# A two-layer attention and feed-forward kernel: scores between gate and up products, attention four query tiles later, values projected in step 15

## The chip, the cores and the metric

The kernel runs on one core of one Trainium2 chip. The metric is the device time of one execution in microseconds (us), median of the runs. TensorE (PE) multiplies matrices out of SBUF into the eight PSUM banks; VectorE (DVE), ScalarE (ACT) and GpSimd (POOL) work on the results; SyncE (SP) issues the DMAs. Each engine executes its own instructions in the order in which they are written, and waits on semaphores where it needs another engine's result.

## The reference

```python
x = L0_attn_x                                     # 4 batches x 512 tokens x 512, f16
xn = _layernorm(x)
s = _L0_attn_ref(xn, Wq, Wk, Wv, Wo)              # 32 query heads, 8 key/value heads of 16, softmax(q k^T / 4) v, then Wo
g = _silu(_L0_ffn_ref(xn, SU_ug, SU_dp, Wscale_ug, Wscale_dp, W_up, W_gate, W_down))
x = x + s * g
...
# _L0_ffn_ref
x = fwht(x * SU_ug) / SCALE
x_up = x @ W_up.T * (Wscale_ug[:INTER] * SCALE)       # INTER = 2048
x_gate = x @ W_gate.T * (Wscale_ug[INTER:] * SCALE)
x = jax.nn.silu(x_gate) * x_up
x = fwht(x * SU_dp) / SCALE
x = x @ W_down.T * (Wscale_dp * SCALE)
```

A second layer follows (a gated linear recurrence and a feed-forward with signs of weights, each again multiplied and added to x). The change touches only layer 0.

## The kernel before

The Walsh-Hadamard transforms are moved onto the weights. Layer 0 is one loop over steps `t` (`TEND` of them), written out once for every engine; `BSTEPS` is 64, so `b, m = t // 64, t % 64` are the batch and the step in it.

**Attention.** A unit `u` is one key/value head of one batch (32 units), with its four query heads. A tile is one unit and 128 query rows: four matmuls (`scores`, one for each query head, 32 rows of contraction, 512 columns) fill the four banks `SC_`; DVE takes the four row maxima (`row_max`, `top_n`), ACT the four exponentials (`exps`, `probs`), SP turns the tile by a DMA transpose (`turn_probs`), and `weigh` multiplies two turned tiles with the values (16 short matmuls). There are 128 tiles, numbered 0 to 127. `scores` of a tile waits until all four exponentials of the tile before have been read out of the banks. After a unit, DVE turns the result (`to_tokens`), divides (`divide`, partly POOL) and, once for two units, turns it back (`to_features`). Before the change tile k stands in step 2k, `weigh` in steps with t % 4 == 0.

**Preparation.** In steps 0 to 31 PE transforms the gate and up weights (`transform_ug`, two f32 products into one of the two banks `GB`), ACT makes the high half (`high_half`), DVE the low half (`low_half`), which frees the bank; POOL does the first level of the butterfly (`chunk_pairs`), four steps to a chunk. The normalised inputs of batches 1 to 3 are turned through one bank `MISC` (`turn_x`, `evict_x`) in the ten steps of `TURN_STEP` from 9 on and in two before. The down weights are taken through butterflies on POOL (`dn_pair`, steps 16 to 61) and through `transform_dn` on PE (the steps `DN_AT`, 49 to 68).

**Gate and up products.** In steps m = 32 to 63 of a batch, `ffn` computes one product per step, eight matmuls of 512 columns into one of the two `GB` banks: even steps gate, odd steps up. ACT takes the tanh of the gate (`tanh_gate`), DVE multiplies (`gate_mul`, which frees the gate's bank, then `up_mul`, which frees the up bank and writes `row32`), ACT copies the high half of `row32` (`high_rows`), POOL writes the low half (`low_rows`), and only then may the next `up_mul` overwrite `row32`. `tanh_gate` waits for the `up_mul` before it, since both use `tg`. `ahead` says how many matmuls of a step's product stand before the scores.

**Down products.** In steps m = 0 to 31 of the next batch (for the last one, t = 256 to 287, with no attention before the change) six matmuls per step; `scale_down`, `tanh_down`, `second_gate`, `project_o` (steps `OUT_STEP`), `gated`, `residual` finish a block of 128 tokens. `project_q`, `project_k` and `project_v` for what comes next use the bank `MISC` too.

**Tail.** At t = 256 SP issues the loads of layer 1 (`tail_constants`: the first batch `nx`, the weights `wst`, eleven constants). At m = 3 of that stretch DVE executes `next_stats`, `weight_max(0)`, `next_scale`, `weight_max(1)` and `weight_maxima` in one piece, each waiting for its load. From m = 11 on SP loads raw weights into `probs`, `probsT` and `rows` (`load_raw`, the first waits for the last `weigh`), ACT writes their signs (`raw_sign`, eight of them), PE turns and projects (`turn_next`, `project_next`), and layer 1 begins when all engines have ended layer 0.

Of the kernel before, what the change touches and what calls it, by code (L numbers as in the profile page):

```python
# [34 lines left out]
TOKEN_STEP, DIVIDE_STEP, TURN_BACK = 4, 6, 2  # L35
GATE_AHEAD, DOWN_AHEAD = (4, 3), (1, 0)
LATE_EVICT = 70
# [3 lines left out]
OUT_STEP = (17, 19, 28, 35)  # L41
OUT_LAST = (17, 21, 28, 35)
NEXT_STEP, EVICT_STEP = 19, 20
XRES_STEP = (17, 19, 24, 25)
Q_STEP, V_STEP, K_STEP = 5, 43, 49
# [112 lines left out]
def layer0(nc, d, x1_dram, W):  # L158

    ctx = ExitStack()  # L160
    with ctx:  # L161
# [113 lines left out]
        def _(sp):  # L275
# [83 lines left out]
            for t in range(TEND):  # L359
                b, m = t // BSTEPS - 1, t % BSTEPS  # L360
                if t % 2 == 0 and 0 <= t // 2 - 1 < NU * TT:
                    turn_probs(t // 2 - 1)
# [11 lines left out]
                if t % STEPS == 6 and t // STEPS + 2 < NU:  # L374
                    load_k(t // STEPS + 2)
                if t % STEPS == 2 and 1 < t // STEPS + 1 < NU:
                    load_q(t // STEPS + 1)
# [15 lines left out]
        def _(pool):  # L393
# [81 lines left out]
            for t in range(TEND):  # L475
# [36 lines left out]
        def _(v):  # L512
# [277 lines left out]
            for t in range(TEND):  # L790
# [27 lines left out]
                if b < B and m > FFN_STEP and m % 2:  # L818
                    gate_mul(b, (m - FFN_STEP) // 2)
                if t % 2 and 0 <= (t - 3 - FFN_STEP) // 2 < LOW_FIRST:  # L820
                    low_rows((t - 3 - FFN_STEP) // 2)
                if t % STEPS == TOKEN_STEP and 0 <= t // STEPS - 1 < NU:
                    to_tokens(t // STEPS - 1)
                if t % STEPS == DIVIDE_STEP and 0 <= t // STEPS - 1 < NU:
                    divide(t // STEPS - 1)
                if t % STEPS == TURN_BACK and 0 <= t // STEPS - 2 < NU and t // STEPS % 2:
                    to_features(t // STEPS - 2)
# [22 lines left out]
        def _(a):  # L850
# [137 lines left out]
            for t in range(TEND):  # L988
# [1633 lines left out]
```

## Time and profile before

| | |
|---|---|
| median of 3 runs | 1391.0 us (1390.41 to 1392.87) |
| profiled execution, its time / its span | 1391.33 us / 1389.4 us |
| busy share over the span | PE 91%, DVE 76%, ACT 56%, POOL 38% |
| granted TensorE clock over the span, of full speed | 0.982 |
| first scores / start of step 32 / start of step 256 / start of layer 1, in the trace | 25.07 / 158.60 / 694.55 / 759.86 us |

Times in the trace count from the span's start. A row of the timeline gives start, length, engine, line, operation, what is written and read, and a count where equal neighbours are merged; in square brackets stands how long the engine was idle before it and whose result ended that. A row of the windows gives, for a stretch, its length and each engine's busy time with the number of its instructions, then the granted TensorE clock, the busy share of the DMA engines and GB/s. A busy PE is an average over stages in which different things end the waits.

### The profile page before, as it was taken

To read this page: it belongs to the slowest core of one execution; us is meant where nothing else is said; L and a number is where in the kernel's file an instruction comes from. 1 tells how busy PE (TensorE), PEld (TensorE's weight loads), DVE (VectorE), ACT (ScalarE), POOL (GpSimd) and SP (SyncE) were. 2 spreads that over 40 slices of the span, in tenths; PEclk is the share of its full clock that TensorE was granted. 3 is DMA by queue.
4 is the path that set the end of the run, shared out by engine and by line. 5 is a ranking of instruction groups with operands and counts; after the bars stand their busy time and mean duration, and the time that the engine had idled before them with its cause. 6 is when DMAs were issued, how large, how long until landed. Compare 5 with 4: busy or idle time off the path is not lost. (4 is left out here: it accounts for less than half of the span.)

```text
span 1389.4 us, 23478 instructions
## 1 busy us (share of the span) xinstructions
PE 1263.2 (91%) x8738; PEld 637.2 (46%) x8738; DVE 1055.3 (76%) x1823; ACT 783.0 (56%) x1308; POOL 524.6 (38%) x434
## 2 busy tenths in 40 slices
PE   4667788888998999998898999999999999999998
PEld 2222233333333333333343555855477555855475
DVE  7765886778887888778863976968956976968946
ACT  5665666666776677667726752355433652355431
POOL 3369865211220132013201663328431573328431
PEclk9898999999999999999999999999999999999999
DMA  6864563577777876877675024001131024001121
GB/s 233 204 143 96 96 107 73 96 145 152 121 117 144 164 122 113 149 160 115 119 260 212 1 59 92 17 31 37 44 72 39 8 59 92 17 31 37 43 43 46
DMA packets 346561, 135.59 MB, mean 98 GB/s; under 512 B 312176, under 2 KB 333392, under 8 KB 343888
## 3 DMA queue, kind: packets, MB, share of 16 engines
q1 hardware_dynamic: 334032, 132.52, 44.1%
q10 hardware_dynamic: 12416, 1.57, 1.0%
q8 instruction: 70, 1.15, 0.4%
q14 instruction: 43, 0.35, 0.1%
HBM read 44.87 MB, written 17.87 MB: 45 GB/s over the span
## 5 line engine op out<-in xcount | busy, mean ns | idle before, releaser
L1157 PE MATMUL bank<-rows,both 128*128 128x512 f16 x1024 | 245.9, 383 | 28.6 <-DVE tg L644 19.8
L638 DVE TENSOR_REDUCE top_n<-vpair 128x1 f32<-128x512 f32 x256 | 164.8, 686 | 102.0 <-PE bank L1126 101.8
L940 ACT ACTIVATE probs<-vpair,top_n 128x512 f16<-128x512 f32 x256 | 164.4, 687 | 109.1 <-DVE top_n L638 109.0
L1171 PE MATMUL bank<-dn,h 128*128 128x512 f16 x768 | 179.8, 383 | 4.3 <-DVE fd L711 2.5
L1157 PEld LDWEIGHTS bank<-rows,both 128*128 128x128 f16 x1024 | 91.3, 98 | 164.8 <-DVE tg L644 43.4
L638 DVE TENSOR_REDUCE top_n<-bank 128x1 f32<-128x512 f32 x256 | 163.7, 682 | 0.0
L940 ACT ACTIVATE probs<-bank,top_n 128x512 f16<-128x512 f32 x256 | 162.9, 690 | 0.0
L454 POOL TENSOR_TENSOR h<-th,h 128x512 f16<-128x512 f32 x61 | 70.5, 1155 | 192.5 <-ACT h L909 192.5
L2239 PE MATMUL bank<-rows,both 128*128 128x512 f16 x512 | 118.5, 382 | 0.0
L1171 PEld LDWEIGHTS bank<-dn,h 128*128 128x128 f16 x768 | 71.5, 99 | 98.3 <-issue 15.9
L2255 PE MATMUL bank<-both,hid 128*128 128x512 f16 x512 | 111.2, 379 | 0.0
L2223 PE MATMUL bank<-rows,both 128*128 128x512 f16 (+1 forms) x456 | 104.0, 379 | 0.9 <-PEq L161 0.9
L2255 PEld LDWEIGHTS bank<-both,hid 128*128 128x128 f16 x512 | 50.0, 98 | 60.5
L467 POOL TENSOR_TENSOR otok<-oblk,rl 128x256 f16<-128x256 f32 x25 | 15.5, 619 | 155.3 <-DVE rl L684 155.3
L2239 PEld LDWEIGHTS bank<-rows,both 128*128 128x128 f16 x512 | 48.4, 100 | 55.5 <-issue 1.1
L909 ACT ACTIVATE h<-th 128x512 f16<-128x512 f32 x64 | 40.3, 629 | 51.5 <-DVE th L657 51.5
L2223 PEld LDWEIGHTS bank<-rows,both 128*128 128x128 f16 (+1 forms) x456 | 43.7, 98 | 55.5 <-issue 4.4
L1614 POOL TENSOR_TENSOR big<-big,both 128x384 f32<-128x384 f32 x32 | 32.0, 1026 | 94.4 <-DMA big<-t_scratch 70.7
L1126 PE MATMUL vpair<-qk 32*128 32x512 f16 x256 | 51.2, 396 | 13.1 <-ACT probs L940 12.9
L1568 POOL TENSOR_TENSOR hid<-sil 128x512 f32<-128x512 f32 x24 | 33.1, 1379 | 62.5 <-DVE sil L1688 62.5
L657 DVE SCALAR_TENSOR_TENSOR th<-bank,hsc,tg 128x512 f32<-128x512 f32 x64 | 48.0, 750 | 9.8 <-DMA x_scratch<-th 6.8
L1628 POOL TENSOR_TENSOR os_<-os_,both 128x6 f32<-128x6 f32 x16 | 23.3, 1458 | 80.6 <-DVE os_ L1986 80.6
(358 smaller groups left out, 2559.3 us busy)
## 6 DMA issues: line engine op xcount, KB each, us to landing
h<-in_ug SPq DMA_DIRECT2D x8, 1024.0 KB, 6.3
lt_scratch<-big SPq DMA_DIRECT2D x16, 384.0 KB, 2.7
dn<-in_down SPq DMA_DIRECT2D x2, 2048.0 KB, 11.0
x_scratch<-th SPq DMA_DIRECT2D x16, 256.0 KB, 2.7
res<-x_scratch SPq DMA_DIRECT2D x16, 256.0 KB, 4.3
out_x<-res SPq DMA_DIRECT2D x16, 256.0 KB, 2.0
both<-in_w SPq DMA_DIRECT2D x2, 1548.0 KB, 11.8
t_scratch<-tok SPq DMA_DIRECT2D x16, 192.0 KB, 2.1
```

The costliest lines, as they stand in the source:

```text
L454: pool.tensor_tensor(h16(ft, 1), row32, h16(ft, 0), ALU.subtract).then_inc(S["row_lo"], 1)
L638: v.tensor_reduce(top_n[:, i:i + 1], SC_[n % G][:, :], AX.X, ALU.max, negate=True).then_inc(S["max_done"], 1)
L657: v.scalar_tensor_tensor(row32, GB[n % 2][:, :], hsc[:, ft:ft + 1], tg[:, :], ALU.mult, ALU.mult).then_inc(S["gb_took"], 1)
L909: a.activation(h16(ft, 0), row32, ACT.Copy).then_inc(S["row_hi"], 1)
L940: a.activation(probs[:, k % TAKEN, j * T:(j + 1) * T], SC_[j][:, :], ACT.Exp, bias=top_n[:, i:i + 1]).then_inc(S["p_ready"], 1)
L1126: pe.matmul(SC_[j][:, :], qs[32 * j:32 * j + 32, u % SLOTS, qt * P:(qt + 1) * P], ks[32 * j:32 * j + 32, u % SLOTS, :], start=True, stop=T ...
L1157: mm = pe.matmul(GB[n % 2][:, :], w[:, kt, col:col + P], xnb(b, kt), start=r == 0, stop=r == 2 * KT - 1)
L1171: mm = pe.matmul(bk, h16(ft, r // 2)[:, rows], dn16(ft, r % 2), start=j == 0 and r == 0, stop=j == FT - 1 and r == 2)
L1568: pool.tensor_tensor(sqf[m % 2], sil[:, ORDER[m], :], sil[:, ORDER[m], :], ALU.mult).then_inc(S["sq_r"], 1)
L2223: mm = pe.matmul(bk, lhs(i, kt), rhs(j, kt), start=n == 0, stop=n == 3 * KT - 1)
L2239: mm = pe.matmul(fbank[ht % 2][:, :], up[:, kt, ht * P:(ht + 1) * P], x_half(i, kt), start=kt == 0 and i == 0, stop=kt == KT - 1 and i == 1)
L2255: mm = pe.matmul(fbank[tt % 2][:, :], hid[:, i, ht, tt * P:(tt + 1) * P], down[:, ht, :], start=ht == 0 and i == 0, stop=ht == HT - 1 and ...
```

## The change

Attention moves by `ATT = 8` steps (four tiles) and by one step in parity: tile k now stands in step 2k + 9, an odd one, between the gate product of the even step and the up product of the odd one. `weigh` stands in steps with t % 4 == 1, there with one up matmul ahead of the scores. The first eight steps hold no attention, and tiles 124 to 127 fall in steps 257 to 263, into the down products of the last batch. In the preparation `transform_ug` goes behind the scores on PE, and `high_half` behind the exponentials and `evict_x` on ACT. `gate_mul` moves between the first and the second row maximum, `up_mul` behind the fourth; `high_rows` goes between the first and the second exponential. `project_v` goes from step 43 to 15, `project_k` from 49 to 57, the output projections from 17 and 19 (17 and 21 for the last batch) to 20 and 22; `evict_q`, `evict_v`, `evict_k` always one step later than their product. No operation is added or dropped.

```diff
+ATT = 8
-TOKEN_STEP, DIVIDE_STEP, TURN_BACK = 4, 6, 2
-GATE_AHEAD, DOWN_AHEAD = (4, 3), (1, 0)
-LATE_EVICT = 70
+TOKEN_STEP, DIVIDE_STEP, TURN_BACK = 6, 0, 2
-OUT_STEP = (17, 19, 28, 35)
-OUT_LAST = (17, 21, 28, 35)
+OUT_STEP = (20, 22, 28, 35)
+OUT_LAST = (20, 22, 28, 35)
-Q_STEP, V_STEP, K_STEP = 5, 43, 49
+Q_STEP, V_STEP, K_STEP = 5, 15, 57
...
@@ SP
-                if t % 2 == 0 and 0 <= t // 2 - 1 < NU * TT:
-                    turn_probs(t // 2 - 1)
+                ta = t - ATT
+                if ta % 2 == 0 and 0 <= ta // 2 - 1 < NU * TT:
+                    turn_probs(ta // 2 - 1)
...
@@ DVE
-                if t > FFN_STEP + 1 and (t - 2) // BSTEPS < B and (t - 2) % BSTEPS >= FFN_STEP and t % 2 == 0:
-                    up_mul((t - 2) // BSTEPS, ((t - 2) % BSTEPS - FFN_STEP) // 2)
-                if t < NU * STEPS and t % 2 == 0:
-                    for j in range(G):
-                        row_max(2 * t + j)
+                ta = t - ATT
+                paired = ta % 2 and 0 <= ta // 2 < NU * TT
+                if paired:
+                    row_max(G * (ta // 2))
+                if b < B and m > FFN_STEP and m % 2:
+                    gate_mul(b, (m - FFN_STEP) // 2)
+                if paired:
+                    for j in range(1, G):
+                        row_max(G * (ta // 2) + j)
+                if t % 2 and 0 <= (t - 3 - FFN_STEP) // 2 < LOW_FIRST:
+                    low_rows((t - 3 - FFN_STEP) // 2)
+                if b < B and m > FFN_STEP and m % 2:
+                    up_mul(b, (m - FFN_STEP) // 2)
...
@@ ACT
                 if b < B and m > FFN_STEP and m % 2:
                     tanh_gate(b, (m - FFN_STEP) // 2)
+                if paired:
+                    exps(G * (ta // 2))
+                if 0 <= fb < B and fm > FFN_STEP and t % 2:
+                    high_rows(fb, (fm - FFN_STEP) // 2)
+                if paired:
+                    for j in range(1, G):
+                        exps(G * (ta // 2) + j)
+                if t in TURN_STEP:
+                    evict_x(KT + TURN_STEP.index(t))
                 if 0 <= t - PREP - 2 < NCH * KT:
                     high_half(t - PREP - 2)
-                if t < NU * STEPS:
-                    exps(2 * t)
-                    exps(2 * t + 1)
-                if t in TURN_STEP:
-                    evict_x(KT + TURN_STEP.index(t))
...
@@ PE
+                ta = t - ATT
+                ahead = 1 if ta % 4 == 1 else 0
                 if t in TURN_STEP:
                     turn_x(KT + TURN_STEP.index(t))
+                ffn(t, 0, ahead)
+                if ta % 2 and 0 <= ta // 2 < NU * TT:
+                    scores(ta // 2)
+                if ta % 4 == 1 and 0 <= ta // 4 - 2 < 2 * NU:
+                    weigh(ta // 4 - 2)
                 if 0 <= t - PREP - 2 < NCH * KT:
                     transform_ug(t - PREP - 2)
-                ahead = 0
-                if t % 2 == 0:
-                    ahead = (DOWN_AHEAD if m < FFN_STEP else GATE_AHEAD)[t // 2 % 2]
-                ffn(t, 0, ahead)
-                if t < NU * STEPS and t % 2 == 0:
-                    scores(t // 2)
-                if t % 4 == 0 and 0 <= t // 4 - 2 < 2 * NU:
-                    weigh(t // 4 - 2)
                 ffn(t, ahead, 2 * KT)
```

On DVE, in the gate and up stretch of the last batch before the change (L638 is `row_max`, L644 `gate_mul`, L657 `up_mul`, L676 `to_tokens`, L684 the reciprocal of `divide`):

```order
L638 TENSOR_REDUCE top_n<-vpair 128x1 x2
L638 TENSOR_REDUCE top_n<-bank 128x1 x2
L676 STREAM_TRANSPOSE oblk<-bank 128x512
L644 SCALAR_TENSOR_TENSOR tg<-tg,bank 128x512
L657 SCALAR_TENSOR_TENSOR th<-bank,hsc,tg 128x512
L638 TENSOR_REDUCE top_n<-vpair 128x1 x2
L638 TENSOR_REDUCE top_n<-bank 128x1 x2
L684 RECIPROCAL rl<-oblk 128x16
L644 SCALAR_TENSOR_TENSOR tg<-tg,bank 128x512
L657 SCALAR_TENSOR_TENSOR th<-bank,hsc,tg 128x512
```

The same place of the changed kernel:

```order
L638 TENSOR_REDUCE top_n<-vpair 128x1
L644 SCALAR_TENSOR_TENSOR tg<-tg,bank 128x512
L638 TENSOR_REDUCE top_n<-vpair 128x1
L638 TENSOR_REDUCE top_n<-bank 128x1 x2
L657 SCALAR_TENSOR_TENSOR th<-bank,hsc,tg 128x512
L676 STREAM_TRANSPOSE oblk<-bank 128x512
L638 TENSOR_REDUCE top_n<-vpair 128x1
L644 SCALAR_TENSOR_TENSOR tg<-tg,bank 128x512
L638 TENSOR_REDUCE top_n<-vpair 128x1
L638 TENSOR_REDUCE top_n<-bank 128x1 x2
L657 SCALAR_TENSOR_TENSOR th<-bank,hsc,tg 128x512
L684 RECIPROCAL rl<-oblk 128x16
```

`gate_mul` no longer stands behind the four maxima and the unit's own operations, but behind the first maximum; the unit's operations stand behind `up_mul`.

On DVE around step 259 (m = 3 of the last stretch), before the change, from the last `up_mul` on (L766 to L734 are `next_stats` to `weight_maxima`, L711 is `scale_down`):

```order
L657 SCALAR_TENSOR_TENSOR th<-bank,hsc,tg 128x512
L766 BN_STATS both<-rows 128x6 x4
L769 BN_AGGR both<-both 128x2 x4
L771 TENSOR_SCALAR both<-both 128x4
L727 TENSOR_REDUCE both<-both 128x1
L776 TENSOR_SCALAR rows<-rows,both 128x512 x4
L727 TENSOR_REDUCE both<-both 128x1
L733 TENSOR_TENSOR both<-both 128x1
L734 TENSOR_REDUCE both<-both 128x1
L676 STREAM_TRANSPOSE oblk<-bank 128x512
L684 RECIPROCAL rl<-oblk 128x16
```

The same place of the changed kernel, from tile 125 on:

```order
L638 TENSOR_REDUCE top_n<-vpair 128x1 x2
L638 TENSOR_REDUCE top_n<-bank 128x1 x2
L766 BN_STATS both<-rows 128x6 x4
L769 BN_AGGR both<-both 128x2 x4
L771 TENSOR_SCALAR both<-both 128x4
L727 TENSOR_REDUCE both<-both 128x1
L776 TENSOR_SCALAR rows<-rows,both 128x512 x4
L727 TENSOR_REDUCE both<-both 128x1
L733 TENSOR_TENSOR both<-both 128x1
L734 TENSOR_REDUCE both<-both 128x1
L638 TENSOR_REDUCE top_n<-vpair 128x1 x2
L638 TENSOR_REDUCE top_n<-bank 128x1 x2
```

The row maxima of tiles 126 and 127, which stood ahead of this piece, now stand behind it.

On PE in steps 10 and 11 of the preparation before the change, from the turn of step 10 on (L1046 is `turn_x`, L1067 and L1068 `transform_ug`, L1126 the scores, L1057 a sum of maxima):

```order
L1046 MATMUL bank<-ident,both 128x128 x4
L1067 MATMUL bank<-h,had 128x512
L1068 MATMUL bank<-h,nhad 128x512
L1126 MATMUL vpair<-qk 128x512 x2
L1126 MATMUL bank<-qk 128x512 x2
L1046 MATMUL bank<-ident,both 128x128 x4
L1067 MATMUL bank<-h,had 128x512
L1068 MATMUL bank<-h,nhad 128x512
```

The same steps of the changed kernel (its lines of PE are eight higher):

```order
L1054 MATMUL bank<-ident,both 128x128 x4
L1075 MATMUL bank<-h,had 128x512
L1076 MATMUL bank<-h,nhad 128x512
L1054 MATMUL bank<-ident,both 128x128 x4
L1134 MATMUL vpair<-qk 128x512 x2
L1134 MATMUL bank<-qk 128x512 x2
L1075 MATMUL bank<-h,had 128x512
L1076 MATMUL bank<-h,nhad 128x512
```

The scores stand in step 11 and ahead of its transform.

## Rows read from the trace of the kernel before

**Rows 1.** Windows: preparation, gate/up and down stretches, the tail.

```profile
25.07:57.66 32.59, 22.52 (x66) 8.46 (x66) 25.24 (x42) 25.39 (x41) 12.15 (x6) 0.90 0.72 234
57.66:158.60 100.94, 69.19 (x295) 25.19 (x296) 66.81 (x116) 60.26 (x104) 74.81 (x57) 0.87 0.61 124
158.60:256.22 97.62, 84.94 (x498) 33.45 (x497) 76.67 (x121) 66.58 (x111) 60.20 (x50) 0.98 0.49 88
325.88:406.57 80.69, 72.99 (x478) 29.18 (x478) 67.85 (x109) 59.94 (x100) 21.93 (x21) 1.00 0.71 125
406.57:470.67 64.10, 58.77 (x407) 23.96 (x408) 49.81 (x84) 43.09 (x70) 6.06 (x8) 1.00 0.81 149
615.15:694.55 79.40, 70.20 (x454) 27.22 (x453) 67.66 (x110) 58.71 (x97) 21.34 (x20) 1.00 0.73 125
694.55:719.24 24.69, 22.20 (x129) 9.87 (x129) 14.49 (x23) 0.65 (x2) 2.71 (x5) 1.00 0.89 303
719.24:759.86 40.62, 35.08 (x168) 15.25 (x168) 21.14 (x34) 26.87 (x21) 5.75 (x6) 0.92 0.53 200
```

**Rows 2.** Who waited for whom, up to 800 us: in total, times, longest.

```profile
ACT probs L940 <- DVE top_n L638: 109.0, 112, 4.7
DVE top_n L638 <- PE bank L1126: 101.8, 106, 3.5
```

**Rows 3.** Timeline of the preparation, about 73 us and 149 us.

```profile
73.41 0.69 ACT L890 ACTIVATE both<-bank,suc 128x512 f16<-128x512 f32 x1 [3.09 <-PE bank L1068]
75.80 0.38 PE L1057 MATMUL bank<-amax,allone 128*128 128x1 f32 x2 [2.42 <-ACT rows L872]
...
149.16 1.13 PE L1067 MATMUL bank<-h,had 128*128 128x512 f32 x2 [1.36 <-DVE both L627]
150.13 1.02 PE L1068 MATMUL bank<-h,nhad 128*128 128x512 f32 x2
```

**Rows 4.** Timeline of one tile's interval in the second gate/up stretch.

```profile
358.33 0.39 PE L1126 MATMUL vpair<-qk 32*128 32x512 f16 x2
358.75 1.29 DVE L638 TENSOR_REDUCE top_n<-vpair 128x1 f32<-128x512 f32 x2 [0.66 <-PE bank L1126]
359.21 2.76 PE L1157 MATMUL bank<-rows,both 128*128 128x512 f16 x12
359.48 1.28 ACT L940 ACTIVATE probs<-vpair,top_n 128x512 f16<-128x512 f32 x2 [0.72 <-DVE top_n L638]
360.66 0.68 ACT L952 ACTIVATE tg<-bank,usc 128x512 f32<-128x512 f32 x1
361.78 0.65 DVE L644 SCALAR_TENSOR_TENSOR tg<-tg,bank 128x512 f32<-128x512 f32 x1
362.47 0.75 DVE L657 SCALAR_TENSOR_TENSOR th<-bank,hsc,tg 128x512 f32<-128x512 f32 x1
362.49 0.82 PE L1157 MATMUL bank<-rows,both 128*128 128x512 f16 x3 [0.52 <-DVE tg L644]
363.24 0.39 PE L1126 MATMUL vpair<-qk 32*128 32x512 f16 x2
363.25 0.63 ACT L909 ACTIVATE h<-th 128x512 f16<-128x512 f32 x1 [0.27 <-DVE th L657]
363.96 1.16 POOL L454 TENSOR_TENSOR h<-th,h 128x512 f16<-128x512 f32 x1 [3.98 <-ACT h L909]
```

**Rows 5.** Timeline of the tail: load of nx, block's end, raw loads, last sign.

```profile
697.40 0.53 SPq L327 DMA_DIRECT2D rows<-x_scratch  x1
710.11 0.45 SPq L345 DMA_DIRECT2D probs<-in_upw  x1
717.07 0.71 DVE L676 STREAM_TRANSPOSE oblk<-bank 128x512 f32<-128x512 f32 x1
719.24 0.61 PE L1171 MATMUL bank<-dn,h 128*128 128x512 f16 x1 [2.49 <-DVE fd L711]
755.25 1.91 ACT L971 ACTIVATE both<-probsT 128x2048 f16<-128x2048 f32 x1 [0.40 <-DMA probsT<-in_downw]
```

More of the change, by code:

```diff
@@ L373, in _ @@
                     load_chunk((t - PREP - 2) // 4 + 2)
[L374 to L377, printed above, removed]
+                if ta % STEPS == 6 and 1 < ta // STEPS + 2 < NU:
+                    load_k(ta // STEPS + 2)
+                if ta % STEPS == 2 and 1 < ta // STEPS + 1 < NU:
+                    load_q(ta // STEPS + 1)
                 if b >= 0 and m in XRES_STEP:
@@ L503, in _ @@
                 fb, fm = (t - 2) // BSTEPS, (t - 2) % BSTEPS
-                if fb < B and fm >= FFN_STEP and t % 2 == 0 and (fb or (fm - FFN_STEP) // 2 >= LOW_FIRST):
+                if fb < B and fm >= FFN_STEP and t % 2 and (fb or (fm - FFN_STEP) // 2 >= LOW_FIRST):
                     low_rows(fb, (fm - FFN_STEP) // 2)
-                if t % STEPS == DIVIDE_STEP and t // STEPS - 1 in POOL_UNITS:
-                    divide(t // STEPS - 1)
+                if (t - ATT) % STEPS == DIVIDE_STEP and (t - ATT) // STEPS - 2 in POOL_UNITS:
+                    divide((t - ATT) // STEPS - 2)
                 if b and m - 2 in out_step(b):
@@ L817, in _ @@
                     bound_scales()
[L818 to L827, printed above, removed]
+                if ta % STEPS == TOKEN_STEP and 0 <= ta // STEPS - 1 < NU:
+                    to_tokens(ta // STEPS - 1)
+                if ta % STEPS == DIVIDE_STEP and 0 <= ta // STEPS - 2 < NU:
+                    divide(ta // STEPS - 2)
+                if ta % STEPS == TURN_BACK and 0 <= ta // STEPS - 2 < NU and ta // STEPS % 2:
+                    to_features(ta // STEPS - 2)
                 if b == B and m == 3:
@@ L993, in _ @@
                     normalise(3)
-                if t > FFN_STEP + 1 and (t - 2) // BSTEPS < B and (t - 2) % BSTEPS >= FFN_STEP and t % 2 == 0:
-                    high_rows((t - 2) // BSTEPS, ((t - 2) % BSTEPS - FFN_STEP) // 2)
+                ta = t - ATT
+                paired = ta % 2 and 0 <= ta // 2 < NU * TT
+                fb, fm = (t - 2) // BSTEPS, (t - 2) % BSTEPS
                 if b < B and m > FFN_STEP and m % 2:
                     tanh_gate(b, (m - FFN_STEP) // 2)
+                if paired:
[7 more added lines that the diff above has]
+                    evict_x(KT + TURN_STEP.index(t))
                 if 0 <= t - PREP - 2 < NCH * KT:
                     high_half(t - PREP - 2)
-                if t < NU * STEPS:
-                    exps(2 * t)
-                    exps(2 * t + 1)
-                if t in TURN_STEP:
-                    evict_x(KT + TURN_STEP.index(t))
                 for ft in range(FT):
@@ L1007, in _ @@
                         magnitudes(ft)
+                if t % 16 == Q_STEP + 1 and t // 16 + 1 < NU // 2:
+                    evict_q(t // 16 + 1)
+                if m == V_STEP + 1 and b + 1 < B:
+                    evict_v(b + 1)
+                if m == K_STEP + 1 and b + 1 < B:
+                    evict_k(b + 1)
                 if t in DN_AT:
                     high_down(DN_AT.index(t))
-                late = 1 if t < LATE_EVICT else 2
-                if t % 16 == Q_STEP + late and t // 16 + 1 < NU // 2:
-                    evict_q(t // 16 + 1)
-                if m == V_STEP + late and b + 1 < B:
-                    evict_v(b + 1)
-                if m == K_STEP + late and b + 1 < B:
-                    evict_k(b + 1)
                 if b and m - 1 in DOWN_END:
```

1 line of the change is left out of this document (added).

## The prediction

> **What bounds the kernel now.** I read the windows by stretch first. Layer 1 (from 759.86 us on) is not touched and starts when layer 0 ends, so only the stretches of [rows 1] count. The reader should see three kinds. In the two stretches of the preparation PE is busy 69% of the time at a granted clock of 0.87 to 0.90 (between its two levels, 1.2 and 2.4 GHz), DVE and ACT 60 to 78%: nobody is full, the steps hang on a ring of waits. In the gate and up stretches PE is busy 88 to 90% and DVE 84%; in a down stretch PE 92%. In the tail PE is full until 716.75 us, waits 2.49 us, and then is busy 86% at clock 0.92. The list of waits, second, says what the ring is: ACT waits 109.0 us for row maxima and DVE 101.8 us for scores [rows 2]: one tile of attention in flight at a time.
>
> The ring of one tile, third, from the timeline [rows 4]. S is the start of a tile's scores. The first row maximum starts at S + 0.42 (358.75), the others 0.60 apart (the second pair starts 1.21 after the first), the first exponential 0.73 after the first maximum, the others 0.60 apart and 0.68 long. Without anything between, the last exponential ends at 0.42 + 0.73 + 3 x 0.60 + 0.68 = S + 3.63, and the next scores can start at S + 3.68. In the row they start at S + 4.91, and not for the exponentials: DVE had four maxima, a unit's operation (0.62 to the next start) and then `gate_mul` (361.78), and PE sat 0.52 us until it freed the gate's bank, then did three matmuls. So before the change a gate/up interval is 0.42 + 4 x 0.60 + unit's operation + 0.65 + 0.05 + three or four matmuls (0.213 apart: 12 take 2.76) with 0.1 behind them: 4.5 to 5.1. The mean is 4.81: the last batch's stretch of 16 tiles is 79.40 [rows 1], 4.96 each, of which I put 2.4 us in all to its start and its one projection.
>
> **Step 1: steps 0 to 7, no attention.** Before, 32.59 us [rows 1]. Left are the transforms: 0.97 + 0.9 = 1.9 us on PE at full clock [rows 3], `high_half` 0.69, `low_half` 0.75, two banks. In the first four steps DVE has the statistics and the first `chunk_max` of about 2.3 each and ACT four normalisations (some 3): I work out 11.4 us; in the next four a chain of 1.9 + 0.69 + 0.75 for two steps and a `chunk_max`, 9.2. Sum 20.6, so **-12**. Bounds: 16 us if only PE's transforms count, 28 if only the exponentials and maxima of four tiles (4.8 us less of waiting) go.
>
> **Step 2: steps 8 to 31.** Before 100.94 us [rows 1], twelve double steps of 8.41. What held them is seen in [rows 3]: ACT idle 3.09 us until PE's transform, then `high_half`, two exponentials, `evict_x`, and PE idle 2.42 us until that `evict_x`: PE and ACT take turns, since ACT has `high_half` ahead of exponentials and `evict_x`. Afterwards scores go ahead of the transform and `evict_x` ahead of `high_half`, so PE transforms while DVE and ACT work on the tile. A double step without turns then takes: first maximum to last exponential 3.20, `high_half` twice 0.69 + 0.60, `low_half` 0.75 (DVE has it ahead of the next maxima), hand-overs 0.15: 5.4; I take 6.0. With turns it is ACT's work: four exponentials 3.1, two `evict_x` 1.2, two `high_half` 1.3, 2.7 magnitudes 1.7: 7.3, I take 7.6. Five double steps with turns, seven without, and 1.0 for each of six chunks (`chunk_max` stands between maxima and `low_half`): 38 + 42 + 6 = 86. So **-15**. Bounds: POOL is busy 74.81 us in this stretch and can't be passed, -26; no gain, 0; a loss is a rival below.
>
> **Step 3: gate and up stretches.** The new ring. DVE has `gate_mul` after the first maximum: 0.60 more, so the exponentials end at S + 4.23 and the scores could follow at S + 4.28; `high_rows` fits in the pause this leaves on ACT. PE: after the scores 0.88 (with `weigh`) or 0.33, then 16 matmuls: 4.2 or 3.8, hidden. The gate was full before the scores, so its tanh (0.68) is done in time. But `up_mul` waits for POOL: first exponential S + 1.14, `high_rows` at 1.74 for 0.63, POOL at 2.45 for 1.16, `up_mul` at 3.65 for 0.75: its bank is free at S + 4.45. Where one up matmul stands ahead of the next scores (every second tile) these start at 4.45 + 0.31 = S + 4.76. A unit's transpose (0.62 in a pause of 0.4) adds 0.24 in three of eight tiles. Mean: (4.28 + 4.76) / 2 + 0.09 = 4.61. Sixteen tiles: 73.8. Three projections, now in steps with `weigh` where PE is full (0.88 + 3.4 + 0.85 + hand-over = 5.3 for 4.28), 1.0 each; output projection 0.4; first double step 1.0. Batches 1 and 2: 78.2 against 80.69, **-2.5** each. Last batch, one projection: 76.2 against 79.40, **-3.2**. Batch 0, 97.62 [rows 1]: the first half gains about 3; in the second `transform_dn` in both steps of a pair makes a ring through `low_rows`, `up_mul`, two `low_down`s of 7.6 us, and `project_k` now stands among them: +2. **-1**. Moving `project_v` out saves nothing more: PE was waiting there for `gate_mul`. Bounds for the mean interval: 4.37 (PE alone with `weigh` half the time) to 4.81, or -15 to +13 us over 64 tiles.
>
> **Step 4: down stretches.** 64.10 us for 16 tiles of 3.68 and projections [rows 1]. The ring is unchanged. `project_v` comes in at m = 15, +0.6; the output projections at 20 and 22 with `project_q` at 21 wait one for the other through `MISC` (`gated` stands behind the maxima of step 21), about 3.6 lost, as much as before. **+0.5** each, three of them: +1.5.
>
> **Step 5: the tail.** T0 is the start of step 256: before, 694.55, and layer 1 starts at T0 + 65.3. Now SP issues the load of `nx` behind the turn of tile 123, 2.85 us after its exponentials as before, at S + 7.1 (S: tile 123, T0 = S + 2.0). DVE's piece of step 259 ended 19.67 us after that issue (697.40 to 717.07 [rows 5]), which nobody but PE's 2.49 us felt. Now the maxima of tile 126 stand behind it: S + 26.8. Scores of tile 127 at S + 26.8 + 3.2 = S + 30. PE could be there at S + 15.2 (three tiles of 3.68, twelve matmuls and `weigh`) and is in order: all down products wait behind, **14.8 us of stall**. Then 54 matmuls and two `weigh`, 13.4, and 1.6 at the lower clock: step 272 at T0 + 43.0, before T0 + 24.7 [rows 1]: +18.3. After that PE had 40.62 us for what, by busy time and clock (35.08 x 0.92), is 32.3 of work; it waited for DVE and ACT, which are now ahead. I take 34.3, 6.3 given back: **+12**. Bounds: +9 (all given back) to +26 (below). The 1.6 is half of the 3.2 us of clock lost in the last window (0.08 x 40), where PE was idle for long twice.
>
> By the Trainium skill, TensorE: Matmul & The Clock Gate (section HAM oscillation — how this bites in real kernels), idle gaps of PE bring the clock down, which speaks against this change; the last window's 0.92 agrees. The page's 426.7 ns against 215.7 ns for 512 columns (section Wait — 56ns, not 53.3ns?) would make it an estimated 2.5 us if the twelve matmuls behind the stall ran slow, and the sum 0.9 higher.
>
> **Sum.** -12 - 15 - 1 - 2.5 - 2.5 - 3.2 + 1.5 + 12 = -22.7. From the profiled execution's own 1391.33 us (span 1389.4 and 1.9 around it; 0.3 above the median): 1368.6, say **1369**.
>
> **Rivals.** *The signs become the end of layer 0.* `load_raw` waits for the last `weigh`, now at S + 43.5. Before, the last sign ended 47.05 us after the first raw load (710.11 to 757.16 [rows 5]) and layer 1 started 2.7 later. Kept whole, that is T0 + 91: +26 for +12, **1383**. Against it: then the first sign had waited for other work, not for its load. *The product ring gains nothing:* `up_mul` through POOL also holds back the tiles without an up matmul ahead, mean 4.81: 64 x 0.20 = +13, **1382**. *Everything fits better:* the interval is PE's 4.37: -15, **1354**. *It doesn't do what it says:* the stretches keep their lengths and tail and start cancel, **1391**. *Slower: the preparation goes serial.* With scores ahead of the transform, at the lower clock: scores to last exponential 3.8, `evict_x` 0.6, turn 0.4, a transform at 1.2 GHz (not quite twice the 1.9) 3.3, `high_half` 0.7, `low_half` 0.75, 9.6 in all per double step, for 7.2, +29: **1398**. It decides against the change above 7.2 + 22.7 / 12 = 9.1 us, more than today's 8.41. For it: clock 0.87 there, and every bank is single. Against: only turns force this order.
>
> **Numbers.** Forecast 0.50 (its own range 1360 to 1378), signs 0.14, product ring 0.10, better 0.09, no change 0.05, serial preparation 0.12. A measurement tells from no change what is above 0.2%, 2.8 us. Faster 0.83, same 0.05, slower 0.12. The range reaches from the better case to beyond the signs: 1354 to 1388.
>
> **What would show it.** First scores about 48 us; step 32 about 131 instead of 158.6; gate/up stretches of 76 to 78; intervals that alternate 4.3 and 4.8; POOL's wait for `high_rows` smaller, `up_mul` waiting for POOL; PE idle about 15 us once in the last 70 us of layer 0, ended by an exponential; lower clock behind it. Wrong it would be made above all by a double step in the preparation far from 7.2, or a tail that keeps all of its 18.

## The result, and the profile after

The changed kernel takes **1399.8 us** (median of 4 runs, 1399.38 to 1404.37), the kernel before 1390.7 beside it. The ratio is 1.0068, 95% interval 1.0046 to 1.0091: slower by 0.7%, where 1369 was predicted. The profiled execution of after took 1404.37 us (span 1402.6), 13.0 more than the one of before and 4.6 above its own median; between the medians lie 9.1.

I cut both traces at the scores of the same steps (of before, tile 16 in step 32, and so on; of after, tile 12 in step 33). The windows of after, with the columns of [rows 1]: preparation, gate and up of batch 0, gate and up of batch 1, down stretch behind it, gate and up of the last batch, and the tail in two parts, up to the scores of tile 127 and to layer 1.

```profile
49.08:135.58 86.50, 62.33 (x281) 25.03 (x280) 65.33 (x112) 61.90 (x107) 72.74 (x54) 0.94 0.52 115
135.58:241.70 106.12, 88.43 (x484) 34.59 (x484) 77.74 (x123) 67.21 (x109) 63.05 (x53) 0.92 0.47 84
315.12:403.01 87.89, 74.90 (x464) 29.91 (x464) 66.19 (x107) 61.13 (x99) 20.29 (x19) 0.94 0.62 114
403.01:469.69 66.68, 59.66 (x423) 24.84 (x425) 50.20 (x86) 43.76 (x72) 7.68 (x9) 1.00 0.79 143
622.75:702.15 79.40, 71.23 (x456) 28.73 (x456) 66.02 (x107) 60.27 (x97) 20.30 (x19) 0.98 0.69 126
702.15:726.02 23.87, 10.15 (x79) 4.15 (x80) 20.61 (x33) 7.89 (x13) 3.32 (x6) 0.85 0.93 278
726.02:772.91 46.89, 46.35 (x258) 20.82 (x258) 26.35 (x44) 29.38 (x25) 5.76 (x5) 0.97 0.69 236
```

The account in us, after less before: start of the first gate and up stretch 135.58 - 158.60 = **-23.0**; gate and up of batch 0 106.12 - 97.62 = **+8.5**, of batch 1 87.89 - 80.69 = **+7.2**, of batch 2 **+6.6**, of batch 3 79.40 against 79.40; the three down stretches +3.8, +2.6, +2.0; from the scores of tile 124 to layer 1 70.76, where before step 256 to layer 1 took 65.31: **+5.4**. Sum +13.1. The preparation gained what was forecast, and everything behind it but the last batch's gate and up stretch lost it again. The +8.5 of batch 0 is partly this one execution: in four other runs that keep its code there (third, sixth, seventh and eighth below) the stretch takes 101.4 to 105.0 us for 106.12. The clock points the same way: 0.94 in batch 1's gate and up stretch, 1.00 before [rows 1].

The list of waits up to 800 us, total, times, longest:

```profile
ACT probs L944 <- DVE top_n L638: 140.9, 131, 13.6
DVE top_n L638 <- PE bank L1134: 70.4, 74, 5.3
ACT kst L920 <- DMA qk<-qst: 19.7, 3, 7.2
```

DVE waits less for scores than in [rows 2], ACT more for maxima. The third row is short and the telling one: three waits of up to 7.2 us, one in each of batches 0 to 2, of `evict_k` for a load of queries. Before, the same three waits came to 3.6 us in all.

Undisturbed tiles run as predicted. Three starts of scores on PE in the second gate and up stretch, `gate_mul` (L644) and `up_mul` (L657, released by POOL's `low_rows`, L454) on DVE between them:

```profile
338.59 0.39 PE L1134 MATMUL vpair<-qk 32*128 32x512 f16 x2
339.62 0.68 DVE L644 SCALAR_TENSOR_TENSOR tg<-tg,bank 128x512 f32<-128x512 f32 x1
342.32 0.75 DVE L657 SCALAR_TENSOR_TENSOR th<-bank,hsc,tg 128x512 f32<-128x512 f32 x1 [0.23 <-POOL h L454]
342.87 0.39 PE L1134 MATMUL vpair<-qk 32*128 32x512 f16 x2
346.59 0.75 DVE L657 SCALAR_TENSOR_TENSOR th<-bank,hsc,tg 128x512 f32<-128x512 f32 x1 [0.22 <-POOL h L454]
347.40 0.39 PE L1165 MATMUL bank<-rows,both 128*128 128x512 f16 x1 [0.58 <-DVE th L657]
347.72 0.39 PE L1134 MATMUL vpair<-qk 32*128 32x512 f16 x2
```

4.28 us from scores to scores, then 4.85 where an up matmul stands ahead of them and waits for `up_mul`, as in the working (4.28 and 4.76). The largest losses lie in single intervals. The first kind, from the scores of tile 57 (m = 59 of batch 1) to those of tile 58, in the timeline of all engines:

```profile
381.59 0.39 PE L1134 MATMUL vpair<-qk 32*128 32x512 f16 x2
382.01 0.69 DVE L638 TENSOR_REDUCE top_n<-vpair 128x1 f32<-128x512 f32 x1 [1.03 <-PE bank L1134]
384.20 2.44 SPq L320 DMA_DIRECT2D qk<-qst  x4
387.96 0.60 ACT L920 ACTIVATE kst<-bank 128x512 f16<-128x512 f32 x1 [7.23 <-DMA qk<-qst]
388.45 0.68 ACT L956 ACTIVATE tg<-bank,usc 128x512 f32<-128x512 f32 x1
389.02 0.69 ACT L944 ACTIVATE probs<-vpair,top_n 128x512 f16<-128x512 f32 x1
389.91 4.02 PE L1165 MATMUL bank<-rows,both 128*128 128x512 f16 x9 [6.09 <-DVE tg L644]
393.86 0.61 PE L1134 MATMUL vpair<-qk 32*128 32x512 f16 x2
```

`evict_k` stands in step m = 58 on ACT and overwrites keys that the loads of heads read; it waits for the last unit's queries, which SP issues in that same step (L320). The tanh of step 59 and the exponentials of tile 57 stand behind it on ACT; DVE waits for the tanh, PE 6.09 us for DVE. Then nine matmuls take 4.02 us, 0.45 each, where twelve undisturbed ones take 2.76, 0.23 each [rows 4]: the clock has fallen (0.75 granted over this interval). The interval is 12.27 us; without the wait it is 4.86 (second experiment). By the Trainium skill, TensorE: Matmul & The Clock Gate (section HAM oscillation — how this bites in real kernels), a PE idle gap is paid a second time through the clock; the trace agrees with these two numbers.

Before the change the eviction was no further from that load in steps: the same step in batch 0, one step behind it in batches 1 and 2. But the four exponentials of tile 57 stood between the two on ACT, and its wait was 1.16 us. In the timeline of before:

```profile
374.29 2.79 SPq L321 DMA_DIRECT2D qk<-qst  x4
375.99 1.27 ACT L940 ACTIVATE probs<-bank,top_n 128x512 f16<-128x512 f32 x2
378.41 0.60 ACT L916 ACTIVATE kst<-bank 128x512 f16<-128x512 f32 x1 [1.16 <-DMA qk<-qst]
```

Now the load is issued behind the turn of tile 56, at 384.20, and ACT has nothing in between: it stands idle from 380.73 on. So by these rows the move laid the wait open by what it took from between the load and the eviction on ACT, not by bringing them into one step.

The second kind, at the first double step of batch 1's gate and up products (timeline):

```profile
318.73 0.58 SPq L388 DMA_DIRECT2D x_scratch<-th  x1
321.52 0.75 DVE L657 SCALAR_TENSOR_TENSOR th<-bank,hsc,tg 128x512 f32<-128x512 f32 x1 [2.90 <-DMA x_scratch<-th]
322.33 3.14 PE L1165 MATMUL bank<-rows,both 128*128 128x512 f16 x8 [2.43 <-DVE th L657]
322.36 0.69 ACT L956 ACTIVATE tg<-bank,usc 128x512 f32<-128x512 f32 x1 [2.51 <-DVE th L657]
```

`up_mul` shares its buffer with the rows of block 2 that are being stored, and now stands in step 33 instead of 34; it waits 2.90 us for the store, and tanh and PE wait for it. With the transposes and the output projection behind it the interval is 9.15 us. This wait is not new. The kernel before has it in the same three stretches, 6.8 us in all for 9.1 here; its row at the start of batch 1's products:

```profile
332.76 0.75 DVE L657 SCALAR_TENSOR_TENSOR th<-bank,hsc,tg 128x512 f32<-128x512 f32 x1 [2.52 <-DMA x_scratch<-th]
```

There the first three intervals of the stretch take 18.0 us, in the changed kernel 18.6.

The tail: load of `nx`, DVE's piece, the maxima of tile 126 behind it, the scores of tile 127, `weight_low`, a tanh of the down products (L964), the first sign.

```profile
703.91 1.12 SPq L326 DMA_DIRECT2D rows<-x_scratch  x1
710.31 2.47 DVE L766 BATCH_NORM_STATS2 both<-rows 128x6 f32<-128x512 f32 x4 [1.14 <-DMA rows<-x_scratch]
722.77 1.28 DVE L638 TENSOR_REDUCE top_n<-vpair 128x1 f32<-128x512 f32 x2
726.02 0.60 PE L1134 MATMUL vpair<-qk 32*128 32x512 f16 x2 [12.65 <-ACT probs L944]
736.50 7.06 DVE L751 SCALAR_TENSOR_TENSOR both<-both 128x1548 f16<-128x1548 f32 x4 [0.94 <-ACT both L969]
747.26 0.63 ACT L964 ACTIVATE th<-fd 128x512 f32<-128x512 f32 x1 [6.27 <-DVE fd L711]
747.80 1.89 ACT L975 ACTIVATE both<-probs 128x2048 f16<-128x2048 f32 x1
```

The stall of tile 127 is there, 12.65 us for the 14.8 predicted; the granted clock over its window is 0.85. What it costs is another question (below).

### The profile page after: what moved, and what is told of

It is laid out like the page before. It is cut to its first block and busy times, and to the rows that moved or that the text cites. A ratio compares the mean times of both kernels' runs of the same rounds, so it can differ in the third digit from the quotient of the medians.

```text
span 1402.6 us, 23475 instructions
## 1 busy us (share of the span) xinstructions
PE 1261.8 (90%) x8738; PEld 642.9 (46%) x8738; DVE 1049.7 (75%) x1823; ACT 787.3 (56%) x1306; POOL 525.1 (37%) x434
## 5 line engine op out<-in xcount | busy, mean ns | idle before, releaser
L1165 PE MATMUL bank<-rows,both 128*128 128x512 f16 x1024 | 252.3, 393 | 40.6 <-DVE th L657 24.6
L944 ACT ACTIVATE probs<-vpair,top_n 128x512 f16<-128x512 f32 x256 | 170.5, 687 | 141.0 <-DVE top_n L638 140.9
L638 DVE TENSOR_REDUCE top_n<-vpair 128x1 f32<-128x512 f32 x256 | 169.3, 682 | 70.8 <-PE bank L1134 70.4
L1165 PEld LDWEIGHTS bank<-rows,both 128*128 128x128 f16 x1024 | 96.5, 100 | 181.7 <-DVE th L657 39.5
L638 DVE TENSOR_REDUCE top_n<-bank 128x1 f32<-128x512 f32 x256 | 163.3, 678 | 0.0
L454 POOL TENSOR_TENSOR h<-th,h 128x512 f16<-128x512 f32 x61 | 70.4, 1155 | 228.8 <-ACT h L913 228.8
L2246 PE MATMUL bank<-rows,both 128*128 128x512 f16 x512 | 118.4, 382 | 0.0
L2246 PEld LDWEIGHTS bank<-rows,both 128*128 128x128 f16 x512 | 48.4, 100 | 55.4 <-issue 0.8
L657 DVE SCALAR_TENSOR_TENSOR th<-bank,hsc,tg 128x512 f32<-128x512 f32 x64 | 48.0, 751 | 22.8 <-POOL h L454 10.5
L956 ACT ACTIVATE tg<-bank,usc 128x512 f32<-128x512 f32 x64 | 43.9, 687 | 37.1 <-DVE th L657 23.4
L1134 PEld LDWEIGHTS vpair<-qk 32*128 32x128 f16 x256 | 12.5, 91 | 91.2 <-ACT probs L944 51.7
```

The costliest lines, as they stand in the source:

```text
L454: pool.tensor_tensor(h16(ft, 1), row32, h16(ft, 0), ALU.subtract).then_inc(S["row_lo"], 1)
L638: v.tensor_reduce(top_n[:, i:i + 1], SC_[n % G][:, :], AX.X, ALU.max, negate=True).then_inc(S["max_done"], 1)
L657: v.scalar_tensor_tensor(row32, GB[n % 2][:, :], hsc[:, ft:ft + 1], tg[:, :], ALU.mult, ALU.mult).then_inc(S["gb_took"], 1)
L944: a.activation(probs[:, k % TAKEN, j * T:(j + 1) * T], SC_[j][:, :], ACT.Exp, bias=top_n[:, i:i + 1]).then_inc(S["p_ready"], 1)
L956: a.activation(tg[:, :], GB[n % 2][:, :], ACT.Tanh, scale=gsc[:, ft:ft + 1]).then_inc(S["tanh_ready"], 1)
L1134: pe.matmul(SC_[j][:, :], qs[32 * j:32 * j + 32, u % SLOTS, qt * P:(qt + 1) * P], ks[32 * j:32 * j + 32, u % SLOTS, :], start=True, stop=T ...
```

## The experiments

"Before" beside the runs had medians of 1389.1 to 1391.3 us. Times are medians.

**First: is it the wait for the last queries, and is the tail's stall the price?** Four kernels, each one edit on the changed one. The first moves `project_k` to step 59, so that `evict_k` stands two steps behind the load:

```diff
-Q_STEP, V_STEP, K_STEP = 5, 15, 57
+Q_STEP, V_STEP, K_STEP = 5, 15, 59
```

> The changed kernel with project_k in step 59 of a batch in place of 57 (its copy in step 60). Theory 1: in the changed kernel ACT's evict_k of step 58 waits until the last queries of the batch have landed, which SP issues only in step 58, and everything behind it on ACT (tanh, exponentials) waits: three intervals of about 12 us instead of 5. Then the three intervals fall to about 5 (one with transforms of down weights around it to about 8) and the kernel gains 15 to 21 us. Theory 2: the 12 us are the price of four more matmuls in a step with weigh, or of the bank MISC: then they move to step 59 unchanged and the time stays within 3 us.

Measured 1389.1 us, ratio 0.9989 (0.9978 to 1.0): 10.7 less than the changed kernel, less than expected but far from the rival. Two of the three waits are left in its trace, 5.5 us together. The second leaves `project_k` alone and has SP load the queries one unit earlier:

```diff
-                if ta % STEPS == 2 and 1 < ta // STEPS + 1 < NU:
-                    load_q(ta // STEPS + 1)
+                if ta % STEPS == 2 and 1 < ta // STEPS + 2 < NU:
+                    load_q(ta // STEPS + 2)
```

> The changed kernel with every unit's queries loaded eight steps earlier (load_q for unit ta // 8 + 2 in place of + 1), project_k stays in step 57. Theory 1 (evict_k waits for the load of the last queries): the three intervals of 12 us fall to about 5 as well, gain 12 to 21 us, with no product moved. Theory 2 (the projection's own place): nothing changes.

Measured **1385.4 us**, ratio 0.9967 (0.9954 to 0.9979): 14.4 less. Interval 57 to 58 is 4.86 us, and the window from tile 44 to 60 is at full clock:

```profile
310.23:389.50 79.27, 71.26 (x463) 29.15 (x463) 66.17 (x107) 61.26 (x99) 20.32 (x19) 1.00 0.70 126
```

79.27 us for 87.89, with `project_k` in the same step. So neither the projection nor its eviction is dear: the wait is.

The third delays DVE's piece for layer 1 behind the maxima of tile 127 (`m == 7` for `m == 3`):

> The changed kernel with DVE's piece next_stats to weight_maxima in step 263 (m = 7), behind the row maxima of tile 127, in place of step 259. Theory: PE's stall of 12.65 us before tile 127 goes; the piece then ends some 4 us later than it does now, so PE stalls 2 to 5 us at step 272, and layer 0 ends 6 to 10 us earlier. Rival: the tail is bound by the signs and raw loads on ACT and SP, whose start hangs on the last weigh: also earlier by about 10, so the gain would be 10 to 13. If the stall was hidden by slack behind it, the gain is under 3 us.

Measured 1400.8 us, ratio 1.0075 (1.006 to 1.009): nothing gained. Three rows of its tail:

```profile
714.49 2.46 DVE L766 BATCH_NORM_STATS2 both<-rows 128x6 f32<-128x512 f32 x4
724.15 1.05 PE L1150 MATMUL bank<-probsT,vaug 128*32 128x256 f16 x16 [9.18 <-issue]
744.88 1.90 ACT L975 ACTIVATE both<-probs 128x2048 f16<-128x2048 f32 x1
```

The tiles follow at 3.7 us now, but PE stands idle 9.18 us ahead of a `weigh` behind them (its row names no releaser; ACT waits there for the turn of a tile, 10.19 us `<-DMA probsT<-probs`), and layer 1 starts 69.43 us after the scores of tile 124 instead of 70.76. My expectation was wrong: taking PE's 12.65 us stall away does not shorten the tail, since the rest of it fills up again.

The fourth puts no up matmul ahead of the scores (`ahead = 0`):

> The changed kernel with no up matmul ahead of the scores in the steps with weigh. Theory (the ring of step 3): the intervals of 4.85 us in the gate and up stretches hang on POOL's low_rows, then up_mul, then the one matmul ahead; without it they fall to 4.3 to 4.4, and the stretches of 16 tiles shorten by 3 to 4 us each, the kernel by 10 to 15. Rival: up_mul's lateness comes out at the next place in the ring (tanh_gate waits for it too), and the time changes by less than 3 us.

Measured 1393.8 us, ratio 1.0024 (1.001 to 1.0037): 6.0 less, about half of what was expected. Gate and up of the last batch is 75.0 us for 79.40.

**Second: the store, the preparation's order, the tail again.** The fifth kernel is the second with the third output projection two steps earlier:

```diff
-OUT_STEP = (20, 22, 28, 35)
+OUT_STEP = (20, 22, 26, 35)
```

> The kernel of the previous experiment with the earlier load of the last queries (1385.4 us), with the third output projection of a block of batches 1 to 3 in step 26 instead of 28, so that its store to x_scratch is issued two steps earlier. Theory (the first up_mul of a batch, now in step 33 instead of 34, waits for the store of block 2 and holds back tanh and scores): the interval of 8.5 to 9.3 us at the start of batches 1 to 3 shrinks by 2 to 3 us each, total 1377 to 1381 us. Rival (the first double step is long because of the projection, the transpose and the second gate themselves, the wait for the store lies beside them): 1384 to 1387 us, intervals unchanged.

Measured **1377.4 us**, ratio 0.991 (0.9884 to 0.9935): 8.0 less than the second kernel. Interval 45 to 46 is 5.54 us, there 8.23, and `up_mul`'s wait for the store is gone from the list.

The sixth puts `transform_ug` ahead of the scores and `high_half` ahead of the exponentials again:

```diff
+                if 0 <= t - PREP - 2 < NCH * KT:
+                    transform_ug(t - PREP - 2)
                 if t in TURN_STEP:
                     turn_x(KT + TURN_STEP.index(t))
                 ffn(t, 0, ahead)
...
-                if 0 <= t - PREP - 2 < NCH * KT:
-                    transform_ug(t - PREP - 2)
```

(and `high_half` on ACT likewise, ahead of the exponentials.)

> The changed kernel with transform_ug ahead of the scores on PE again and high_half ahead of the exponentials and evict_x on ACT, as before the change; tiles still four later. Theory (the prediction's step 2: about 13 us of the preparation's gain of 25 come from this order, the rest from steps 0 to 7 without attention): the start of step 32 comes 10 to 15 us later than the changed kernel's, total 1410 to 1415 us. Rival (the whole gain comes from the tiles that are four later and no longer stand beside the start, the order matters nothing): within 2 us of the changed kernel, 1398 to 1402 us.

Measured 1422.7 us, ratio 1.0239 (1.0221 to 1.0256): 22.9 more, twice what was expected. The window from its first scores to tile 12:

```profile
50.07:161.31 111.24, 73.87 (x276) 28.99 (x277) 64.89 (x111) 62.36 (x106) 72.71 (x56) 0.80 0.40 88
```

111.24 us for 86.50, at clock 0.80 for 0.94. The list of waits from 45 to 135 us names it. Of the sixth kernel:

```profile
ACT both L894 <- PE bank L1076: 36.0, 17, 4.4
```

And of the changed one, where `high_half` on ACT waits a third as long for the transform:

```profile
ACT both L894 <- PE bank L1076: 12.6, 11, 1.9
```

The seventh has the tail's `weight_low`, 7.06 us of DVE, in steps 18 to 21 instead of 12 (one of four in each):

> The changed kernel with the four weight_low of the tail (7.06 us of DVE in one piece) in steps 18 to 21 of the last stretch, one per step, instead of all in step 12. Theory (in the tail DVE's queue sets the end: it is busy without a pause from the first maxima of tile 126 to the tanh that the signs stand behind): tanh and signs come 5 to 7 us earlier, total 1394 to 1397 us. Rival (PE, busy without a pause from the end of its 12.65 us stall to the end of layer 0, sets the end): within 2 us of the changed kernel, 1398 to 1402 us.

Measured 1407.2 us, ratio 1.0124 (1.0107 to 1.0141): 7.4 *more*. Its timeline, the end of `weight_low` on DVE and the first sign on ACT:

```profile
745.77 7.05 DVE L751 SCALAR_TENSOR_TENSOR both<-both 128x1548 f16<-128x1548 f32 x4
752.91 1.91 ACT L974 ACTIVATE both<-probs 128x2048 f16<-128x2048 f32 x1 [7.79 <-DVE both L751]
```

The first sign overwrites what `weight_low` reads. Neither theory held, but the run shows the link: the signs can't start before DVE's `weight_low` has ended.

The eighth is the third with the eleven constants of layer 1 loaded in step 266 instead of 256, behind the turns of the last tiles on SP's queue:

> The changed kernel with DVE's piece for layer 1 in step 263 instead of 259 (as in the experiment on the tail before, 1400.8 us) and the eleven constants of layer 1 loaded in step 266, behind the turn of tile 127, instead of in step 256. Theory (DVE's queue sets the end of layer 0): the remaining 9.2 us for which PE waited for a turned tile go away, but the total stays within 3 us of the changed kernel, 1397 to 1402 us. Rival (PE's idle time is the price): layer 1 starts 8 to 10 us earlier, 1390 to 1392 us.

Measured 1400.5 us, ratio 1.0082 (1.0064 to 1.01). PE's idle time ahead of `weigh` is 6.62 us for 9.18, and layer 1 starts 70.34 us behind the scores of tile 124. It did not remove the wait, only shortened it, so by itself it decides little; with the third it says that two stalls of PE can shrink and the end stays.

**Third: parts alone on the kernel before, and the edits together.** The ninth is the kernel before with `V_STEP` 15 and nothing else:

> The kernel before the change with one number changed: the values of the next batch are projected in step 15 of a batch instead of step 43. Theory (the prediction's steps 3 and 4: 0.6 us more in each of three down stretches, nothing saved in the gate and up stretches, where PE waited for gate_mul anyway): 1390 to 1394 us. Rival (the projection cost the gate and up stretch its whole 2 to 3 us each): 1383 to 1387 us.

Measured 1400.7 us, ratio 1.007 (1.005 to 1.0089): **9.4 more**; both theories missed. Of that the trace (1396.4 us) shows 5.3 in the preparation and 1.3 in each of two down stretches. First its preparation, then 25 us of it from just behind the moved projection (at 92.20 us) on:

```profile
24.66:163.47 138.81, 95.35 (x375) 36.30 (x375) 90.47 (x158) 86.33 (x146) 87.18 (x62) 0.83 0.61 145
94.98:120.36 25.38, 15.14 (x55) 5.52 (x55) 10.46 (x16) 12.47 (x22) 17.39 (x13) 0.66 0.39 92
```

In its timeline there:

```profile
98.56 0.38 PE L1046 MATMUL bank<-ident,both 128*128 128x128 f16 x4 [2.64 <-ACT vaug L930]
101.90 0.69 ACT L890 ACTIVATE both<-bank,suc 128x512 f16<-128x512 f32 x1 [3.48 <-PE bank L1068]
```

`turn_x` waits for `evict_v` through `MISC`, ACT for the transform behind it. PE has three more waits of 2.4 to 2.7 us in this window, for `evict_x`; the granted clock over it is 0.66.

The tenth is the kernel before with only the preparation's new order (`transform_ug` behind scores and `weigh`, `high_half` behind `evict_x`):

> The kernel before the change, tiles where they were (even steps, no shift), with only the preparation's order of the change: transform_ug behind scores and weigh on PE, high_half behind the exponentials and evict_x on ACT. Theory (the order is the whole gain of the preparation, wherever the tiles stand): start of step 32 about 20 to 26 us earlier, 1365 to 1371 us. Rival (the order gains only together with a tile that has all its exponentials in one step and eight steps without attention ahead of it): 1380 to 1392 us, start of step 32 at 148 us or later.

Measured **1374.3 us**, ratio 0.9886 (0.9867 to 0.9906): 17.0 less, with no shift of the tiles, somewhat short of the 20 to 26 expected. The window of its preparation:

```profile
21.75:139.33 117.58, 86.44 (x364) 35.78 (x365) 92.39 (x162) 87.25 (x150) 80.00 (x55) 0.92 0.71 173
```

And that of the kernel before:

```profile
25.07:158.60 133.53, 91.70 (x359) 33.65 (x360) 92.06 (x158) 85.65 (x145) 86.97 (x62) 0.88 0.63 151
```

Step 32 starts 19.3 us earlier. The eleventh has the queries early, the third projection in step 26 and `ahead = 0`:

> The changed kernel with the last queries of a batch loaded one unit earlier, the third output projection in step 26, and no up matmul ahead of the scores (the three edits of earlier runs together: 14.4 us, 8 us and 6.0 us, each against the kernel that it was made on). Theory (the three are separate waits and add up): 1370 to 1374 us, gate and up stretches of batches 1 and 2 about 74 us. Rival (they share one wait): 1376 to 1379 us.

Measured **1365.7 us**, ratio 0.9814 (0.9798 to 0.983), 34.1 less than the changed kernel where the three edits gave 14.4 + 8.0 + 6.0 = 28.4. The windows of batch 1's and the last gate and up stretch:

```profile
309.21:383.04 73.83, 70.16 (x462) 29.52 (x463) 66.08 (x107) 61.51 (x99) 20.32 (x19) 1.00 0.73 136
589.48:661.81 72.33, 68.53 (x454) 28.65 (x455) 65.98 (x107) 60.42 (x97) 20.32 (x19) 1.00 0.76 134
```

PE is busy 95% there. The waits were separate; why they give 5.7 more together I did not trace.

The twelfth is the eleventh with `weight_scales` ahead of `next_split` on DVE:

> The combined kernel with weight_scales ahead of next_split on DVE in step 265. Theory (the end of layer 0 is one chain: load of nx, DVE's piece, two tiles' maxima, next_split, weight_scales, weight_high on ACT, weight_low on DVE, tanh, eight signs, layer 1): ACT's weight_high starts 3.8 us earlier, weight_low is released earlier, and the time from the scores of tile 124 to layer 1 shrinks by 2.5 to 3.8 us against the combined kernel. Rival (PE or the loads of the raw weights set that end): less than 1 us.

Measured 1365.6 us, ratio 0.9825 (0.9804 to 0.9847): nothing. ACT's `weight_high` starts 3.4 us earlier, counted from the scores of tile 124 (690.89 - 661.67 = 29.22, in the eleventh 694.40 - 661.81 = 32.59), `weight_low` only 0.6 (33.57 for 34.21). The two rows of its timeline:

```profile
690.89 6.01 ACT L969 ACTIVATE both<-both 128x1548 f16<-128x1548 f32 x4
695.24 1.82 DVE L751 SCALAR_TENSOR_TENSOR both<-both 128x1548 f16<-128x1548 f32 x1
```

DVE has to do `next_split` before it either way, so an earlier hand-over through ACT releases nothing.

**Fourth: does `V_STEP` 15 cost in the changed kernel too?** On the changed kernel, then on the eleventh, each with `V_STEP` 43:

> The changed kernel with the next batch's values projected in step 43 again. Theory (the projection in step 15 costs about 5 us in the preparation, where its eviction holds the single bank and the clock falls, and 1.3 in each of two down stretches, as it does in the kernel before): 1390 to 1394 us, the preparation from first scores to step 33 some 3 to 5 us shorter. Rival (in the changed kernel the order of the preparation hides it, and in step 43 the gate and up stretches, with PE full in steps of weigh, take 1 to 2 us more each): 1399 to 1403 us.

> The combined kernel (1365.7 us) with the next batch's values projected in step 43 again. Theory as in the run beside it: 1356 to 1361 us. Rival: 1365 to 1369 us.

Measured 1403.0 us, ratio 1.0101 (1.0083 to 1.0119), and 1367.3 us, ratio 0.9841 (0.9823 to 0.9859). Both lie above their partners with `V_STEP` 15, by 3.2 and 1.6 us, with intervals that overlap: the rival. In the new order of the preparation `V_STEP` 15 costs nothing that shows; in the old order it cost 9.4.

## Why the prediction was wrong

- **Steps 1 and 2, the preparation: sum right, split wrong, and so partly luck.** Forecast -27; the first gate product starts at 130.58 us instead of 156.78, -26.2. The order of step 2 gives 19.3 by itself on the kernel before (137.51, tenth kernel), where I had 15. The shift of the tiles, step 1's -12, adds less. Where the pairs differ in the tiles' place and agree in `V_STEP`, the product comes 8.8 us earlier in the new order (128.72 in the thirteenth kernel, 137.51 in the tenth) and 3.7 in the old one (157.94 in the sixth, 161.65 in the ninth). Each is one execution of each kernel, and other runs of the changed kernel's order and `V_STEP` start that product anywhere from 129.96 to 134.23. That the sixth kernel starts it no earlier than the kernel before, 157.94 for 156.78, is the `V_STEP` 15 that it also holds.
- **Step 3, the failed one: "three projections ... 1.0 each" and "first double step 1.0".** I priced `project_k` as 0.85 us of PE in a full step and its eviction at a hand-over. On ACT that eviction now follows the exponentials of a tile at once, while SP has yet to issue the load that it waits for, and tanh and exponentials are queued behind it. One wait of 5.6 to 7.2 us in each of three batches, plus the clock: 14.4 us by the second kernel, which is faster than the kernel before. So this wait is what made the change slower. The first `up_mul` waits for the store of block 2: 8.0 us in three batches by the fifth, where I had 1.0 each. The kernel before waits for the same store (6.8 us in its list), which I had not read; this is a term of my sum that was too small, not a new cost of the change. Without the two, gate and up of batches 1 and 2 are 76.6 us, under my 78.2, and the last one is 75.6 for 76.2. So the ring was right and the stretches without the two waits no longer than forecast; two waits on DMAs were missing. The sum of the two, 22.4, is most of the 30.8 between forecast (1369) and measurement.
- **Batch 0** stays high: 100.3 us without the wait for queries and 104.8 in the fifth kernel's profile, forecast 96.6. I had seen the ring of `transform_dn` and priced it too low; its parts were not tried apart.
- **Step 4, down stretches:** +3.8, +2.6, +2.0 for +0.5 each. The two output projections take one interval of 6.69 us, 3.0 above the 3.68 of an undisturbed one, near the 3.6 of the working and no more than they cost before. The rest was not traced.
- **Step 5, the tail: stall right, price by another chain.** Stall 12.65 us for 14.8; from step 256 to layer 1 the tail is 8.1 us longer for 12. But the stall is not why. From the start of DVE's piece to the first sign it took 31.05 us before (704.13 to 735.18), 37.49 in the changed kernel with the maxima of two tiles inside, 30.39 in the third, where they are ahead of it and the piece starts later. From first sign to layer 1: 24.7, 25.1, 24.7. DVE's work in order up to a `scale_down` behind `weight_low`, the tanh that waits for it ahead of the first sign (6.27 us, row above), then eight signs, sets the end; the last signs wait about 1 us each for raw loads, before and after. That this is the cause was shown by two misses (third and twelfth kernel) and the release in the seventh, not by a version in which DVE has less to do.
- **The rivals.** "Slower" ended on the right side, but for a preparation gone serial, which didn't happen. "The signs" named the right end of the chain and the wrong start of it (`load_raw`). No rival held a load on the queue of SP against an eviction on ACT. Once the two waits' 22.4 are taken off, 8.4 of the 30.8 are left. By the trace they lie in batch 0 and the down stretches, with the tail on the other side of the account; no run took them apart, and their cause stays open.

## What to carry to other kernels

When an operation is moved, list for every engine what it waits for *at its new place*, DMAs issued in the same step above all, and what is queued behind it: the same eviction cost 14.4 us here and waited for nothing once its load was issued a unit earlier. An order of two engines that hand one bank to and fro is worth trying by itself before anything is shifted: it gave 17.0 us on the kernel before, and the shift of the tiles came out below that only with its DMAs arranged (1365.7 us). What the shift itself is worth is open: no run put the earlier store, whose wait the kernel before has too, on the tenth kernel. And a stall of PE is not a price until the end moves: 12.65 us of it could be taken away and gained nothing, since other work set the end.

## What was not expected of the hardware

A wait costs more than its length through the clock. The three waits of `evict_k` sum to 19.7 us of ACT; PE's granted clock over the interval shown was 0.75, and a stretch that held one ran at 0.94 instead of 1.00. Short waits go with a low clock too: in the ninth kernel no wait of PE in the window of 25 us is longer than 2.7 us, and the granted clock over it is 0.66. The order alone lifted the preparation's clock from 0.88 to 0.92 (tenth kernel), and taking it back lowered it from 0.94 to 0.80 (sixth).
